# Projections around a norm, earlier weight loads and separate banks for last rows in a four-layer attention kernel

## The reference

```python
x = out + hidden_state                                   # end of layer 1
x = (x - mu) * rsqrt(var + 1e-6) * gamma + beta
...
h = _layer_norm(x, ln1_scale, ln1_offset)                # layer 2
qh = (h @ wq1 + bq1); kh = (ctx @ wk1 + bk1); vh = (ctx @ wv1 + bv1)
weights = softmax(qh kh^T / sqrt(128)); x = x + (weights vh) @ wo1 + bo1
h = _layer_norm(x, ln2_scale, ln2_offset)                # and the same again with wq2, wk2, ...
```

## Time and profile before

| | |
|---|---|
| median of 3 runs | 4368.75 us (4366.56 to 4369.88) |
| the profiled execution | 4369.97 us, its span 4368.2 us |
| PE busy | 3996.6 us (91%) |
| DVE, ACT, POOL busy | 2560.6, 1861.7, 1216.4 us |
| mean granted clock of PE | 0.966 |

### The profile page before, as it was taken

One profiled execution on the slowest core, in us unless ns is written; L12 is line 12 of the kernel. 1 busy time (PEld: TensorE's weight loads), 2 busy tenths in 40 slices (PEclk: granted clock), 3 DMA queues, 4 the chain that ended last, 5 costly groups with the idle time before them and its releaser, 6 DMA issues. The chain is left out here.

```text
span 4368.2 us, 55253 instructions
## 1 busy us (share of the span) xinstructions
PE 3996.6 (91%) x21018; PEld 2971.9 (68%) x21018; DVE 2560.6 (59%) x4130; ACT 1861.7 (43%) x3290; POOL 1216.4 (28%) x1326
## 2 busy tenths in 40 slices
PE   6899799998999989998878997999989999899988
PEld 5655488887888877543765555888878888775437
DVE  2588655565655665455525885565556556655555
ACT  2487444343434431455124883443434434314541
POOL 1543223132222313221215422131322223132213
PEclk9899899999999999999889998999999999999999
DMA  2211111110101102221222211010111111132212
GB/s 69 59 37 25 44 32 35 32 44 30 36 22 44 39 30 87 55 57 29 80 77 64 38 19 49 27 44 22 44 34 32 34 33 39 39 92 49 49 30 89
DMA packets 167573, 195.62 MB, mean 45 GB/s; under 512 B 18627, under 2 KB 123272, under 8 KB 167310
## 3 DMA queue, kind: packets, MB, share of 16 engines
q1 hardware_dynamic: 142734, 151.15, 11.2%
q0 software_dynamic: 24576, 40.94, 4.9%
HBM read 149.02 MB, written 2.10 MB: 35 GB/s over the span
## 5 line engine op out<-in xcount | busy, mean ns | idle before, releaser
L1321 DVE TENSOR_TENSOR w_pt_lo<-ps,w_pt_hi 128x512 fp32r<-128x512 f32 x512 | 334.8, 685 | 157.6 <-ACT w_pt_hi L1252 157.5
L1097 POOL CAST w_wo_hi<-w_raw 128x1024 fp32r<-128x1024 f32 x32 | 33.2, 1037 | 1328.8 <-PE ps L148 1323.1
L1252 ACT ACTIVATE w_pt_hi<-ps 128x512 fp32r<-128x512 f32 x512 | 281.2, 595 | 203.7 <-PE ps L1189 203.7
L897 DVE CUSTOM_DVE_ANT_0 g_units<-ps,g_mask 128x1024 f32<-128x1024 f32 x256 | 311.1, 1217 | 81.2 <-PE ps L760 81.1
L1733 ACT ACTIVATE h_pt<-ps,zero_col 128x512 f32<-128x512 f32 x384 | 257.1, 686 | 233.6 <-PE ps L1689 232.3
L1782 DVE TENSOR_REDUCE h_mxs<-ps 128x1 f32<-128x512 f32 x384 | 243.8, 684 | 160.0 <-PE ps L1678 158.3
L1304 DVE TENSOR_REDUCE w_mx<-ps 128x1 f32<-128x1024 f32 x256 | 312.0, 1219 | 33.6 <-PE ps L148 33.0
L1189 PE MATMUL ps<-ident,w_p 128*128 128x128 f32 x2048 | 279.1, 275 | 39.5 <-DVE w_pt_lo L1321 39.5
L772 PE MATMUL ps<-ident,g_units 128*128 128x128 f32 x2048 | 290.8, 283 | 20.3 <-ACT g_turned L851 18.1
L843 ACT ACTIVATE g_units<-g_units,g_nmx 128x1024 f32<-128x1024 f32 x256 | 294.5, 1151 | 17.9 <-DVE g_nmx L897 15.2
L1189 PEld LDWEIGHTS ps<-ident,w_p 128*128 128x128 f32 x2048 | 235.4, 140 | 96.0 <-DVE w_pt_lo L1321 66.5
(11 more groups left out here) (358 smaller groups left out, 10246.7 us busy)
## 6 DMA issues: line engine op xcount, KB each, us to landing
w_raw<-in_L_xattn_wk SPq DMA_DIRECT2D x32, 512.0 KB, 3.4
w_raw<-in_L_xattn_wq SPq DMA_DIRECT2D x32, 512.0 KB, 3.5
w_raw<-in_L_xattn_wv SPq DMA_DIRECT2D x32, 512.0 KB, 3.7
w_raw<-in_L_xattn_wo SPq DMA_DIRECT2D x32, 512.0 KB, 3.6
mlp_raw<-in_L_xattn_w_fc SPq DMA_DIRECT2D x64, 256.0 KB, 3.1
mlp_raw<-in_L_xattn_mlp_w SPq DMA_DIRECT2D x64, 256.0 KB, 3.1
h_ks<-h_k_hi POOLq DMA_DIRECT2D x64, 192.0 KB, 3.0
g_qs<-g_q_hi POOLq DMA_DIRECT2D x256, 32.0 KB, 1.9
```

The lines of the kernel that those rows point to most:

```text
L897: dve.tensor_tensor_reduce(units[:, q % U, :].rearrange("p (h w) -> p h w", h=2), ps[:, 2 * (q % 2):2 * (q % 2) + 2, :], mask[:, q % 4, :] ...
L1252: act.activation(pt.h[:, x[2] % 4, :], ps[:, T_BANK + tn % 2, :], ACT.Copy).then_inc(t_hi, 1)
L1321: dve.tensor_tensor(pt.l[:, x[2] % 4, :], ps[:, T_BANK + tn % 2, :], as_f32(pt.h[:, x[2] % 4, :]), ALU.subtract).then_inc(t_free, 1)
```

## The change

- `grouped`: the four last output groups go to banks 0 to 3 (the score banks) and not to the ring's bank. PE waits once for all scores to be read, and no more for the add before. SP and POOL take no part in its barrier.
- `norm` n1: SP issues the k and q weights of the coming wide stage when the last score has been read (the mask's memory is then free), then waits for the last product with `turned` and issues gamma and beta, which get memory inside the 52 KB set aside. POOL splits k when the scores are read, and q and v when the last turns are done; v no more waits for n_xn.
- `norm` n1 and n2: `pe_early` runs k.0.0 and k.0.1 before the turns and k.1.0 and k.1.1 behind them, ahead of the barrier.
- `wide`: q.0 of the first chunk goes to bank 0 (SA).
- `latent`: the last fold goes to bank 4, the four last output groups to banks 0, 1, 2, 3, after all scores and exponentials are done, and their turn in the ring falls away.

```diff
-            done = new_barrier()
+            done = new_barrier(3)
...
+            def ring_of(x):
+                return ps[:, x[2], :] if x[0] == "o" and x[1] == C - 1 else ring
...
             def ring_turn(pe, b, x):
-                if ring_at[x]:
+                if x[0] == "o" and x[1] == C - 1:
+                    pe.wait_ge(s_free, (b + 1) * STEPS)
+                elif ring_at[x]:
...
-                barrier(sp, done, b)
...
-                barrier(pool, done, b)
...
-            TA, TB = 2, 3
+            TA, TB, SA = 2, 3, 4
             early = {("k", 0, 0): A, ("k", 0, 1): BB, ("k", 1, 0): TA, ("k", 1, 1): TB}
+            first_banks = {**early, ("q", 0): SA}
...
+            def sp_weights(sp, b, name, c=0):
+                i, g = "kqvo".index(name), (b * 2 + nth) * C + c
+                upto(sp, split, g * 4 + i - 1)
+                sp.dma_start(raw_of(i, name), view(name)[c, :, :, :]).then_inc(loaded[i % 2], 16)
+
             def sp_(sp, b):
                 r = b * 2 + nth
                 for c in range(C):
                     g = r * C + c
                     for i, name in enumerate("kqvo"):
-                        upto(sp, split, g * 4 + i - 1)
-                        sp.dma_start(raw_of(i, name), view(name)[c, :, :, :]).then_inc(loaded[i % 2], 16)
+                        if nth or c or i > 1:
+                            sp_weights(sp, b, name, c)
...
-                        elif name == "v":
-                            pool.wait_ge(sem("xn_done"), b * norms[0] * LT + LT)
+                        elif name == "k":
+                            pool.wait_ge(sem("g_scores_free"), (b + 1) * 128)
+                        else:
+                            for h in range(2):
+                                pool.wait_ge(sem(f"g_turn_full{h}"), (b + 1) * 128)
...
-            def pe_early(pe, b):
-                for x in early:
-                    pe_k(pe, b * 2 + nth, 0, x)
+            def pe_early(pe, b, u):
+                for h in range(2):
+                    pe_k(pe, b * 2 + nth, 0, ("k", u, h))
...
-            ahead_of = dict(zip(early[8:], early)) | dict(zip(late[1:], late))
+            ends = [("fold", C - 1)] + [("o", C - 1, lt) for lt in range(LT)]
+            bank_of |= dict(zip(ends, (T_BANK_ + 1, 0, 1, 2, T_BANK_)))
+            ahead_of = dict(zip(early[8:], early)) | {x: y for x, y in zip(late[1:], late) if x not in ends}
...
+                if x in ends:
+                    pe.wait_ge(s_free, (b + 1) * HEADS * LT * HF)
+                    pe.wait_ge(e_done, (b + 1) * HEADS * KT)
...
                 if first:
+                    sp.wait_ge(sem("g_scores_free"), (b + 1) * 128)
+                    for name in "kq":
+                        first_weights[tag](sp, b, name)
+                    sp.wait_ge(sem("g_pv_done"), (b + 1) * 64)
                     for i in range(2):
                         sp.dma_start(gb[:, i, :], first[i].unsqueeze(0).broadcast_to([P, D])).then_inc(rows_ld, 16)
...
                 if tag in ahead_in:
-                    ahead_in[tag](pe, b)
+                    ahead_in[tag](pe, b, 0)
                 for lt in range(LT):
...
                             i.then_inc(turned, 1)
+                if tag in ahead_in:
+                    ahead_in[tag](pe, b, 1)
                 barrier(pe, done, b)
```

More of the change, by code:

```diff
@@ L41 @@
 AHEAD = 52 * 1024
+GAMMA_AT = 44 * 1024
 ENGINES = 5
@@ L812, in pe_ @@
                                 pe.wait_ge(split["o"], g + 1)
-                            i = mm3(pe, ring, att[:, lt * P:(lt + 1) * P], wo[:, :], True, True)
+                            i = mm3(pe, ring_of(x), att[:, lt * P:(lt + 1) * P], wo[:, :], True, True)
                         i.then_inc(ring_full, 1)
@@ L928, in dve_ @@
                             ring_wait(dve, b, x)
-                            dve.tensor_tensor(X[:, x[2], :], ring, X[:, x[2], :], ALU.add).then_inc(o_added, 1)
+                            dve.tensor_tensor(X[:, x[2], :], ring_of(x), X[:, x[2], :], ALU.add).then_inc(o_added, 1)
                 barrier(dve, done, b)
@@ L986, in wide @@
             work, turns, hi_of, xo_of = {}, {}, {}, {}
-            last_in, ahead_of, ends = [None] * 4, {}, {}
+            last_in, ahead_of, ends = [None] * 5, {}, {}
             for s_ in [(0,) + x for x in early] + in_steps:
@@ L991, in wide @@
                 if key in banks and (c, key) not in work:
-                    bk = work[c, key] = banks[key] if c else {**banks, **early}[key]
+                    bk = work[c, key] = banks[key] if c else {**banks, **first_banks}[key]
                     ahead_of[c, key], last_in[bk] = last_in[bk], (c, key)
@@ L1030, in bank @@
             def bank(c, key):
-                return ps[:, (R_BANK, R_BANK + 1, T_BANK, T_BANK + 1)[work[c, key]], :]
+                return ps[:, (R_BANK, R_BANK + 1, T_BANK, T_BANK + 1, S_BANK)[work[c, key]], :]
             def wait_freed(eng, r, c, key):
@@ L1361, in dve_ @@
                 barrier(dve, done, b)
-            ahead_in["n" + i_] = pe_early
+            ahead_in["n" + i_], first_weights["n" + i_] = pe_early, sp_weights
             add(sp_, pool_, pe_, act_, dve_)
@@ L1828, in build @@
         norms = [0, 0]
-        ahead_in = {}
+        ahead_in, first_weights = {}, {}
         def norm(tag, src, eps, c_scale, c_shift, rms=False, first=None):
             own = ExitStack()
-            sb(own, tag + "_next_stage", [P, AHEAD // 4])
+            if first:
+                sb(own, tag + "_next_weights", [P, GAMMA_AT // 4])
+                gb = sb(own, tag + "_gb", [P, 2, D])
+                sb(own, tag + "_next_stage", [P, (AHEAD - GAMMA_AT) // 4 - 2 * D])
+            else:
+                sb(own, tag + "_next_stage", [P, AHEAD // 4])
             xn = sb(own, tag + "_xn", [P, LT, D])
@@ L1838, in norm @@
             ve, sd, rs = (sb(own, tag + n, [P, LT]) for n in ("_ve", "_sd", "_rs"))
-            gb = sb(own, tag + "_gb", [P, 2, D]) if first else None
             rows_ld = sem(tag + "_rows_loaded") if first else None
```

## The result

The changed kernel takes 4317.27 us, the median of 4 runs (4313.70 to 4323.02), beside 4369.32 (4366.56 to 4379.63) for the kernel before: a ratio of 0.9883, 95% interval 0.9870 to 0.9896. The profiled execution took 4314.76, its span 4313.0 against 4368.2, its mean granted clock 0.975 against 0.966. So the saving is 52 us by the medians and 55 by the profiled executions; the forecast was 54.

The account below looks back on a forecast made before the run. TensorE is busy most of the span, so gains lie only in seams where it stands still. Savings of 11.2 (latent attention), 17.2 (seam 2) and 25.7 (seam 1) sum to 54.1 us, giving about 4314.7; range 4303 to 4331.

Parts of the forecast that it names:

- Last output rows: End of the 32-head attention: with four banks, 5.4 us from first output matmul to last add, a saving of 3.55.
- Latent end: End of the latent attention: four banks save 3.55, the fold in its own bank 2.05, together 5.6 us a batch.
- No wait for beta, and the long steps: First norm on DVE: beta's wait goes, 1.90 us less; n_xn and X take 2.75 for four, not 3.52 and 7.49.
- Rival B: Loads or POOL's splits come too late and lie beside the norm again; 4322 us, chance 0.08.
- The lock: Seam 1: att_lo on DVE waits out POOL's q subtraction, 1.8 us lost once a batch, ending 0.54 after it.
- Rival C: DVE's att_lo starts first or POOL is late by half a microsecond: 3.6 us less, 4311; chance 0.09.
- Seam 2: Second norm, first early projection to DVE sum on v.0: 18.9 us, from 26.82 and 28.17; 17.2 saved in all.
- Rival A: In all four norms the projections behind the turns run wholly at 1.2 GHz: 16 us, 4331; chance 0.11.
- The barrier: At the norm's barrier, before q.0, PE arrives last: crossing taken as 0.35 us, bounds 0.1 and 1.0.
- Seam 1: Attention to wide stage, first output matmul to DVE sum on v.0: 36.7 us, from 48.54 and 50.62; 25.7 saved.
- the last four turns 0.6: Seam 1, after n_xn: only four of the turns remain on the path, 0.6 us, between 0.48 and twice that.
- Rival D: Slower than before: shifted PE starts or waits in wide-stage chunks draw more low-clock stretches, 4395 at 32 chunks; chance 0.02.

## Why the prediction was right

The direction, the size and nearly all steps held; the time came out 2.6 us above 4314.7, and the profiled execution 1.1 below the forecast of 4315.9 for it. The three sums of the forecast were 11.2, 17.2 and 25.7, and 11.6, 16.8 and 24.8 were measured, 53.2 in place of 54.1. That they came so near is the reasoning's merit. That the whole time did is in part luck: stretches where nothing was changed gave 4.6 us back and saved 6.6.

- Last output rows. Last add 5.27 us after the first matmul in batch one (480.78 to 486.05), forecast 5.4, the adds at most 1.28 apart. In the kernel with the banks only it is 5.49, with the adds 1.28 apart.
- Latent end. 6.06 and 5.50 against 5.6 each. In batch one the last matmuls of the twelve ran at the upper level, inside the bound that the forecast gave as up to 1.6 more.
- No wait for beta, and the long steps at 2.73 and 2.74 for four: as forecast. Rival B (cover gone) did not occur; POOL's k and q splits end 10 us before n_xn; v's, which had to wait for its DMA, began at 484.51 and was over before n_xn too.
- The lock. 1.58 against 1.8, once a batch, and ending 0.55 after POOL's subtraction, forecast 0.54; the subtraction itself ended at 480.13 and not 481.9, with DVE as much earlier. The kernel with POOL held back showed it to be the cause. The Trainium skill (SBUF — State Buffer, "Who interferes with whom") gives the rule: a VectorE instruction with two SBUF inputs and a GpSimd instruction that reads SBUF shut each other out for whole instructions. The rows agree, 2.33 in place of 0.75. Rival C (no lock) therefore falls as an outcome.
- Seam 2: 19.08 from the first projection to the v.0 sum against 18.9, term by term 5.58 to the turns (5.55), 1.67 for them (1.9), 6.01 for 24 projections and the barrier (5.9), 5.82 for q.0 and v.0 (5.6). Saved 16.8, forecast 17.2. Rival A (the projections behind the turns wholly at 1.2 GHz) did not occur.
- The barrier, which had no row: 0.26 of idle before q.0, inside the bounds of 0.1 and 1.0. v.0 found its bank free.
- Seam 1: 24.8 against 25.7. With the lock counted it is 37.30 against 36.7.

The one step of seam 1 that was mis-sized is "the last four turns 0.6". From the end of n_xn (501.41) to the first projection behind the turns (503.43) it is 2.02. In its sum the forecast gave the low clock behind the gap to the 24 projections and none to the turns, though these come first after it; it also put the end of the first two projections at about 497 and the pause at some 5 us, where it is 7.42. Its own terms give some 7.5: last add at 487.96, projections from 488.9 to 494.4, the first part of n_xn ready at 502.0. Its bound (0.48 to 0.96) allowed for the lower level, but only for four turns. At that level PE fell behind DVE: all 16 took 3.33 us from start to start (500.10 to 503.43), and only 1.31 of these had passed when n_xn was ready. The projections in turn were a little cheaper, 7.26 with the barrier against 7.85, and so the two errors met in part.

What was missing altogether is how the low-clock stretches behind the seams change. Rival D named the mechanism, but as a disaster of 22 chunks or more with a chance of 0.02. On a small scale it occurred: four wide stages hold five low stretches before the change and seven after, and take 4.6 us more. The largest part is behind seam 2 of batch two, where the seam itself went as forecast (before, then after):

```profile
3261.64:3788.98 527.34, 506.51 (x2862) 428.33 (x2862) 314.07 (x504) 218.04 (x416) 129.83 (x80) 1.00 0.11 31
...
3213.37:3744.29 530.92, 509.99 (x2862) 431.33 (x2862) 314.70 (x504) 218.18 (x416) 134.31 (x83) 0.99 0.11 31
```

Since one kernel had such a stage with and without them, a single profile doesn't show that the change called them.

What stays open: why the stretches that no edit touches differ by some microseconds from one execution to the next, and why in one batch out of ten the turns ran slow after a pause under 2 us.

## What to carry to other kernels

When independent work can stand on either side of a step that waits, ask for each place on its own on which side the engine idles: at the first norm PE waits 7.4 us before the turns, and three or four projections there beat two, while at the second it never waits and two on each side save 6.7 us a batch. A seam that gets shorter is not yet a faster kernel: compare also the granted clock of the stage behind it, which was up to 4 us longer or shorter for the same work, and profile a kernel more than once before a difference of a few microseconds outside the seams is put down to an edit. Price an overlap by its whole instruction when two SBUF inputs on DVE meet POOL, and do not add up parts that shorten the same chain: in seam 1, 32 us of single savings made 25 together.

## What the runs showed of the hardware

The turns show what a pause does. At n1, after 4.66 to 7.42 us without a matmul, the 16 turns took 3.43 to 3.68 us in 10 batches out of 10; after 1.45 to 1.92 they took 2.02 or 2.03 in 9 out of 10, and 3.51 in one; after 0.38, in one batch, 2.03; with none, 1.91.

Low stretches also come late. In the changed kernel two of them, some 3 us long each, lie 3 and 20 us behind the v.0 sum of seam 1. PE is busy throughout each, but each begins 1 to 1.5 us behind a wait of PE: 2.14 us for the first, 1.21 for the second. In the windows view of every kernel here, two batches each, the length of the stage behind seam 1 goes by their number alone: none, 527.4 to 527.9 us (10 batches); one, 529.0 to 529.7 (7); two, 530.6 to 531.6 (9). A low stretch there costs about 1.7 us. The stage behind seam 2 shows the same: none, 527.2 to 528.2 (13 batches); one, 529.1 to 529.9 (4); two, 530.6 to 531.7 (9).

With four projections before n1's turns, early weights and separate banks there was none behind seam 1, in 8 batches out of 8; with two on each side, in the two profiled executions of the changed kernel, there were two in 4 out of 4. The order alone doesn't decide it: the kernel with the weights early and nothing else has four before the turns too, and had two stretches in one batch (531.0) and none in the other (527.9). Behind seam 2 of batch two the kernel with four before n1 had two in one execution and none in the other, with the same waits of PE (2.14, 1.7 and 1.2 us) in both. What calls a stretch so late was not shown.
